# A fused two-layer transformer step: one attention key per query tile goes from TensorE to VectorE in layer 0's tiles 9 to 14

## What is computed

```python
scores = jnp.einsum('bqd,bkd->bqk', Qr, Kr) / jnp.sqrt(jnp.float32(d))
mask = jnp.tril(jnp.ones((T, T), dtype=bool), k=1)
scores = jnp.where(mask[None, :, :], scores, -jnp.inf)
attn = jax.nn.softmax(scores, axis=-1)
out = jnp.einsum('bqk,bkd->bqd', attn, V)
```

## Time and profile before

| | |
|---|---|
| median of 3 runs | 727.2 us (727.04 to 727.38) |
| profiled execution, its time | 725.66 us |
| its span in the trace | 723.9 us |
| PE busy | 640.5 us (88%) |
| PEld busy | 497.7 us (69%) |
| DVE busy | 473.1 us (65%) |
| ACT busy | 341.8 us (47%) |
| POOL busy | 225.4 us (31%) |
| granted TensorE clock, mean | 0.974 |

### The profile page before, as it was taken

One profiled execution on the slowest core, in us unless ns is written; L12 is line 12 of the kernel. 1 busy time (PEld: TensorE's weight loads), 2 busy tenths in 40 slices (PEclk: granted clock), 3 DMA queues, 4 the chain that ended last, 5 costly groups with the idle time before them and its releaser, 6 DMA issues.

```text
span 723.9 us, 10992 instructions
## 1 busy us (share of the span) xinstructions
PE 640.5 (88%) x3840; PEld 497.7 (69%) x3858; DVE 473.1 (65%) x1258; ACT 341.8 (47%) x705; POOL 225.4 (31%) x247
## 2 busy tenths in 40 slices
PE   5788899998878989988899998968889997899996
PEld 4356687877656778774668786846678885576774
DVE  5956499675767557726569776586744436766665
ACT  1133454565535464543445465443555552554553
POOL 3325545453544211004555445264410002000000
PEclk9979999999989999999999999998999999999999
DMA  8400000000000000000000000000000000001001
GB/s 261 117 1 1 1 2 1 1 2 0 1 1 1 0 1 1 1 1 1 1 0 2 0 1 1 1 1 1 1 1 1 2 2 0 1 15 30 15 24 34
DMA packets 12077, 9.64 MB, mean 13 GB/s; under 512 B 1708, under 2 KB 10744, under 8 KB 12024
## 3 DMA queue, kind: packets, MB, share of 16 engines
q1 hardware_dynamic: 12024, 8.94, 4.2%
HBM read 6.84 MB, written 2.10 MB: 12 GB/s over the span
## 4 chain that ended last, share of the span: by engine, by line
PE 65%; DVE 16%; ACT 8%; POOL 7%; issue 4%; DMA 1%; SPq 0%; POOLq 0%; ACTq 0%; DVEq 0%
PE ps L787 14%; PE ps L657 12%; PE ps L765 8%; PE ps L936 4%; PE ps L938 4%; PE ps L937 4%; PE ps L616 4%; PE ps L810 2%; PE ps L675 2%; PE ps L811 2%; PE ps L826 2%; ACT xn L1053 2%; DVE xn L1339 1%; PE ps L838 1%; DVE xn L1258 1%
## 5 line engine op out<-in xcount | busy, mean ns | idle before, releaser
L1113 ACT ACTIVATE probsT<-ps 128x512 f32<-128x512 f32 (+3 forms) x160 | 85.3, 533 | 172.1 <-PE ps L765 172.1
L787 PE MATMUL ps<-v_sb,probsT 128*128 128x129 f32 (+1 forms) x1148 | 157.1, 280 | 3.7 <-ACT probsT L1115 3.7
L787 PEld LDWEIGHTS ps<-v_sb,probsT 128*128 128x128 f32 (+1 forms) x1148 | 141.5, 191 | 10.7 <-ACT probsT L1115 5.6
L1376 DVE TENSOR_REDUCE row_max<-ps 128x1 f32<-128x512 f32 (+2 forms) x144 | 88.2, 620 | 61.3 <-PE ps L657 26.3
L765 PE MATMUL ps<-ident,probs 128*128 128x128 f32 (+1 forms) x574 | 92.6, 278 | 14.6 <-ACT hT L1043 7.8
L1087 ACT ACTIVATE probs<-ps,neg_max 128x512 f32<-128x512 f32 (+7 forms) x158 | 92.7, 617 | 15.8 <-DVE neg_max L1383 12.0
L765 PEld LDWEIGHTS ps<-ident,probs 128*128 128x128 f32 (+1 forms) x574 | 65.4, 139 | 45.6 <-issue 41.8
L515 POOL TENSOR_TENSOR hq<-ha,hp 128x352 f32<-128x352 f32 x32 | 29.9, 933 | 128.7 <-DVE hp L1419 128.7
L657 PE MATMUL ps<-k_high,q_high 128*128 128x512 f32 (+4 forms) x110 | 44.9, 408 | 2.3 <-ACT probs L1087 2.2
L1188 ACT ACTIVATE probs<-ps 128x512 f32<-128x512 f32 x40 | 24.0, 599 | 44.8 <-PE ps L938 44.8
L1391 DVE RECIPROCAL rsum<-ps 128x1 f32<-128x1 f32 x64 | 10.5, 165 | 50.3 <-PE ps L787 50.1
(11 more groups left out here) (243 smaller groups left out, 1376.7 us busy)
## 6 DMA issues: line engine op xcount, KB each, us to landing
out<-x_sb SPq DMA_DIRECT2D x8, 256.0 KB, 2.3
x_sb<-in_L_attn_x SPq DMA_DIRECT2D x2, 512.0 KB, 5.5
hT_all<-in_L_wmod SPq DMA_DIRECT2D x2, 384.0 KB
rope_cos<-table_cos SPq DMA_DIRECT2D x1, 768.0 KB, 6.8
rope_sin<-table_sin SPq DMA_DIRECT2D x1, 768.0 KB, 8.3
rope_cos<-table_cos SPq DMA_DIRECT2D x1, 256.0 KB, 3.6
rope_sin<-table_sin SPq DMA_DIRECT2D x1, 256.0 KB, 4.9
moe_raw<-in_L_ffn_expert_gate_w SPq DMA_DIRECT2D x1, 256.0 KB, 3.9
```

Source lines behind the costliest of these rows:

```text
L787: mm = pe.matmul(bank(OUT_AT, 0, V_W), probsT[0:size, n % 4, k * P:(k + 1) * P], v_sb[0:size, j, :], start=(c == 0 and k == 0), stop=(c == ...
L1113: ins = act.activation(probsT[:, n % 4, 0:full], bank(TURN, 0, full), ACT.Copy)
L1376: ins = dve.tensor_reduce(dst, ps[:, start:start + width], AX.X, ALU.max, negate=single)
```

## The change

For layer 0's tiles 9 to 14 (`edge_by_vector`; slots 9 to 14 of both batches, 12 in all) the key beyond the diagonal is no longer a tile of its own.

- Scores: where the last chunk is shorter than a bank (tiles 9, 10, 12, 13, 14) its three products and its mask product are two columns wider, and the four products of two columns go. Tile 11's last chunk fills its bank, so its four extra products stay.
- Turn and values: the transpose of one column, ScalarE's copy of one partition and the two products over one row go. Tile 11 has three chunks instead of four.
- finish(s) gets one VectorE instruction before the reciprocal: on partitions 96 to 127, value row times probability added to the accumulator in PSUM (129 columns), linked by a semaphore, and a wait for `v_edge_loaded`.
- The value rows lie on partition 127 of `v_edge`, a view of `moe_raw`, which GpSimd zeroes (128 x 1032 fp32) behind `first_rsqrt(2)`. SyncE moves them by four DMAs of one partition (2 KB), two for each batch, each behind a wait for the values and for the DMA before it.
- ScalarE waits for these DMAs before it puts layer 1's values over layer 0's (line 1011).
- SyncE's six loads of the experts' weights now stand behind these DMAs and behind layer 0's last tile of batch 1.

```diff
+EDGE_FROM = 9
+def edge_by_vector(layer, i):
+    return layer == 0 and EDGE_FROM <= i < TILES - 1
 def turn_chunks(layer, i):
     tiles = [(j, P) for j in range(i + 1)]
-    if layer == 0 and i < TILES - 1:
+    if layer == 0 and i < EDGE_FROM:
         tiles.append((i + 1, 1))
...
+            sp.wait_ge(edge_zeroed, 1)
+            for b in range(BATCH):
+                for g in range(EDGE_TILE // GROUP, GROUPS):
+                    sp.wait_ge(v_ready, b * 2 * GROUPS + g + 1)
+                    if b and g == EDGE_TILE // GROUP:
+                        sp.wait_ge(x_attn, (b - 1) * SLOTS + TILES)
+                    done = b * (GROUPS - EDGE_TILE // GROUP) + g - EDGE_TILE // GROUP
+                    if done:
+                        sp.wait_ge(v_edge_loaded, 16 * done)
+                    tiles = slice(g * GROUP - EDGE_TILE, (g + 1) * GROUP - EDGE_TILE)
+                    sp.dma_start(v_edge[P - 1:P, tiles, :], v_sb[0:1, g * GROUP:(g + 1) * GROUP, :]).then_inc(v_edge_loaded, 16)
+            EDGES = BATCH * (GROUPS - EDGE_TILE // GROUP)
+            sp.wait_ge(v_edge_loaded, 16 * EDGES)
+            sp.wait_ge(x_attn, (BATCH - 1) * SLOTS + TILES)
...
             first_rsqrt(2)
+            pool.memset(v_edge[:], 0.0).then_inc(edge_zeroed, 1)
...
-                mm = products(slice(start, start + full), not last)
+                beyond = 2 if width > full else 0
+                within = beyond if full < BANK and edge_by_vector(layer, i) else 0
+                mm = products(slice(start, start + full + within), not last)
                 if last:
-                    mm = pe.matmul(ps[:, start + full - P:start + full], ident_b[:],
-                                   (mask0, mask1)[layer][:, 0:P], start=False, stop=True)
-                    if width > full:
+                    mm = pe.matmul(ps[:, start + full - P:start + full + within], ident_b[:],
+                                   (mask0, mask1)[layer][:, 0:P + within], start=False, stop=True)
+                    if beyond > within:
...
+                if n % (2 * GROUPS) >= GROUPS:
+                    act.wait_ge(v_edge_loaded, 16 * (GROUPS - EDGE_TILE // GROUP) * (n // (2 * GROUPS) + 1))
                 act.wait_ge(v_proj_ready, n + 1)
...
                     acc = bank(OUT_AT, 0, V_W)
+                    if edge_by_vector(layer, i):
+                        per_batch = GROUPS - EDGE_TILE // GROUP
+                        dve.wait_ge(v_edge_loaded, 16 * (b * per_batch + (i + 1) // GROUP - EDGE_TILE // GROUP + 1))
+                        edge = acc[EDGE, :]
+                        link(dve.scalar_tensor_tensor(out=edge, in0=v_edge[EDGE, i + 1 - EDGE_TILE, :],
+                                                      scalar=probs[EDGE, s % 2, (i + 1) * P:(i + 1) * P + 1],
+                                                      in1=edge, op0=ALU.mult, op1=ALU.add))
                     link(dve.reciprocal(rsum[:, s % 2:s % 2 + 1], acc[:, P:V_W]))
```

More of the change, by code:

```diff
@@ L180, in build @@
         moe_raw = sb("moe_raw", [P, 3 * UNITS, P])
+        EDGE_TILE = EDGE_FROM // GROUP * GROUP
+        EDGE = slice(P - 32, P)
+        v_edge = moe_raw[:].rearrange("p n d -> p (n d)")[:, 0:(TILES - EDGE_TILE) * V_W].rearrange(
+            "p (t n) -> p t n", n=V_W)
         wv_s = sb("wv_s", [P, BATCH, P])
@@ L301, in build @@
         fp4_w_loaded = sem("fp4_w_loaded")
+        edge_zeroed = sem("edge_zeroed")
+        v_edge_loaded = sem("v_edge_loaded")
         moe_w_loaded = sem("moe_w_loaded")
@@ L659, in products @@
                     return mm
-                mm = products(slice(start, start + full), not last)
+                beyond = 2 if width > full else 0
+                within = beyond if full < BANK and edge_by_vector(layer, i) else 0
+                mm = products(slice(start, start + full + within), not last)
                 if last:
-                    mm = pe.matmul(ps[:, start + full - P:start + full], ident_b[:],
-                                   (mask0, mask1)[layer][:, 0:P], start=False, stop=True)
-                    if width > full:
-                        beyond = slice(start + full, start + full + 2)
-                        products(beyond, False)
-                        mm = pe.matmul(ps[:, beyond], ident_b[:], mask0[:, P:P + 2], start=False, stop=True)
+                    mm = pe.matmul(ps[:, start + full - P:start + full + within], ident_b[:],
+                                   (mask0, mask1)[layer][:, 0:P + within], start=False, stop=True)
+                    if beyond > within:
+                        alone = slice(start + full, start + full + 2)
+                        products(alone, False)
+                        mm = pe.matmul(ps[:, alone], ident_b[:], mask0[:, P:P + 2], start=False, stop=True)
                 mm.then_inc(scores_ready, 1)
```

## The result

| | before | after |
|---|---|---|
| median | 727.3 us (4 runs, 727.0 to 728.5) | 715.4 us (4 runs, 714.3 to 718.3) |
| profiled execution, its time | 725.66 us | 714.27 us |
| its span | 723.9 us | 712.4 us |
| mean granted TensorE clock in it | 0.974 | 0.978 |

The ratio of the times is 0.985 (95% interval 0.9825 to 0.9873): 11.9 us less, where 6.7 were forecast. In short: the work that the change takes off the path came out at 7.6 us, near the forecast 6.7; the rest, some 4 us, lies where TensorE spent less time at its lower clock, for which the forecast had allowed 1.7.

What follows compares the result with a forecast made beforehand. PE bounds the kernel (65% of what ended last), filling nearly all of slots 10, 11, 13 and 14. Two batches of 3.69 less, 0.65 more for the setup: 6.7 less, 727.2 to 720.5 us; range 718.2 to 723.6.

Steps and rivals of the forecast that it cites:

- Prices on PE: Work removed from PE: two-column score products 0.38 us, one-column turn 0.11, pair of one-row value products 0.51.
- The rival of cheap one-row products: Value products: one-row pair worth only its issue, 0.22 us instead of 0.51; 722.8 us in all, chance 0.12.
- Slots 8 and 9: No gain: VectorE still starts behind GpSimd's L507, so PE waits for xq at 118.06 whatever it saves.
- Slot 12: Gain of 0.42 us a batch; its value products hidden under normalise_2, VectorE's added instruction covered by up to 0.84.
- Slot 14: Net gain of 0.50 us a batch: 0.72 on PE less 0.22 because VectorE starts q_low late.
- The added instruction: VectorE in each finish: 0.35 us, bounds 0.28 and 0.69, plus 0.05 for link and wait.
- The memset: Setup: GpSimd's memset, about 0.88 us, blocks VectorE's L1295; 0.65 more taken, bounds 0 and 0.65.
- Moved loads, row DMAs: SyncE's moved expert loads cost zero; row DMAs come five slots early, so waits for them cost zero.
- The clock: Rival in layer 1's short slots: one TensorE clock fall more or fewer, 1.7 us, 719 to 722; chance 0.12.
- The rival on the slower side: Longer PE waits in slots 10 and 12 to 14 cost the clock: 6.8 to 13.6 us, up to 734.1; chance 0.06.

Runs made afterwards that it cites:

- e3: Changed kernel with the score products of before back in all tiles, so the values part alone; median 720.8 us, ratio 0.9905.
- e2: Kernel before with the score part alone (wider last chunks), value row still through TensorE; median 723.3 us, ratio 0.9956.
- e8: Changed kernel without VectorE's added instruction, the waits kept and the value row left out of the result; a single run, 713.9 us.
- e1: Changed kernel run again with no edit; median 714.7 us, ratio 0.9855.
- e7: Changed kernel with the memset moved ahead of first_rsqrt(1), where VectorE is idle; median 714.8 us, ratio 0.986.
- e12: Changed kernel with one setup instruction issued twice, to shift everything behind it by 1.36 us; median 716.9 us, ratio 0.9865.
- e6: Changed kernel with filling products in TensorE's idle times to hold the clock; median 711.6 us, ratio 0.980.
- e10: Changed kernel with clock-holding filling products, eight more ahead of slot 10, and the memset moved early; median 711.0 us, ratio 0.978.
- e11: Kernel before with one setup instruction issued twice, to shift everything behind it by 1.36 us; median 727.9 us, ratio 1.0007.
- e4: Kernel before with only the memset and SyncE's moved loads added; median 727.15 us, ratio 1.0001.
- e5: Kernel before with filling products in TensorE's idle times to hold the clock; median 717.95 us, ratio 0.990.

## Why the prediction was wrong, point by point

- **Prices on PE: right, a little low.** The end of slot 11 fell from 2.87 to 1.76, forecast 1.82. Slots 10, 11 and 13 came out at -0.81, -1.08, -0.98 for -0.72, -1.05, -1.00. Slots 10 and 14 each gave 0.08 to 0.09 more: fourteen products and the seam take 1.48 (124.80 to 126.28), 0.106 a step where I used 0.112. The rival of cheap one-row products (0.29 less gain in each of four slots) is refuted by e3's slot steps.
- **Slots 8 and 9: mis-sized, 0 instead of 0.25.** I asked only whether VectorE's conversion (line 1417 before, 1458 after) would get in before GpSimd, and it did not: 1.29 again. I overlooked what stands ahead of it. GpSimd's L507 took 1.52 because, it seems, the VectorE instruction ahead (L1414, from 106.58) ran beside its first part. After, VectorE is some 0.25 earlier against GpSimd, and the same GpSimd instruction takes 1.27. First DVE of before, then DVE and POOL of after, slot 8:

```profile
106.58 0.52 DVE L1414 SCALAR_TENSOR_TENSOR ha<-silu_g,qh 128x352 f32<-128x352 f32 x1
```

```profile
105.42 0.53 DVE L1455 SCALAR_TENSOR_TENSOR ha<-silu_g,qh 128x352 f32<-128x352 f32 x1
...
105.80 1.27 POOL L537 TENSOR_TENSOR xn<-xn,mod_row_now 128x512 f32<-128x512 f32 x1 [1.76 <-ACT xn L1087]
...
105.98 1.29 DVE L1458 TENSOR_SCALAR hp<-ha 128x352 int32<-128x352 int32 x1
```

  The 0.25 goes on through VectorE's wait and GpSimd's xq to PE. That L1414 is what lengthened it is argued from the overlap; e2 and e3 show that it comes with the scores part alone (1.27 in e2, 1.50 in e3). The wait ahead of slot 10 is 1.84 for a forecast 1.9.
- **Slot 12: mis-sized, -0.24 for -0.42.** I had called the added instruction covered there by up to 0.84. It was, but for the statistics' last step, which slipped behind the start of a GpSimd instruction and was held 0.33 longer; e8 gives 0.16 back. Also, the slots are not independent there, as the wait for ScalarE at slot 12's end takes back what slots 10 and 11 gave beyond the forecast: counted from slot 10, 2.19 were forecast up to there and 2.13 came.
- **Slot 14: mis-sized, -0.75 for -0.50.** q_low was to start 0.22 late. PE's wait grew by 0.11 (1.07 to 1.18) and 0.06 came back just ahead of it, so VectorE charged 0.05. The order of the queue was as described; the instructions ahead of q_low fitted better.

```profile
158.83 0.38 DVE L1429 SCALAR_TENSOR_TENSOR ps<-moe_raw,probs,ps 32x129 f32<-32x129 f32 x1
...
160.43 0.67 DVE L1410 TENSOR_REDUCE row_max<-ps 128x1 f32<-128x512 f32 x1
...
161.02 0.68 DVE L1507 SCALAR_TENSOR_TENSOR q_low<-ps,q_high 128x512 fp32r<-128x512 f32 x1
```

- **The added instruction: right.** 0.38 in all twelve places, for 0.35.
- **The memset: right in kind and size.** It took 0.96 for 0.88, and the tensor_scalar beside it 0.80 for a forecast 0.85, so it is no exception for writing only. That agrees with the rule of the Trainium skill ("SBUF — State Buffer", "Who interferes with whom"). The forecast's bound, 17.3 + 0.1 - 16.78, is 0.62 and not 0.65; 0.6 came.
- **Moved loads, row DMAs: right, nothing.** SyncE's longest wait on a row DMA was 1.1 us, and no other engine waited for one.
- **The clock: the step that failed.** The sum held no term for it, and the range allowed for one fall more or fewer, 1.7 us, in layer 1's slots. That was mis-sized. By the slots and the memset alone the time would have been 719.6, inside the range; the changed kernel came out another 3.1 us lower by the means of all runs and some 4 by the medians and by the two profiled executions. In those, the falls in the setup, at slot 18 and at the turn of the batches were moved, shorter or missing, worth about 4 us together, and in e1's those in the setup and at slots 18 and 25 of batch 1. Before's own 56 runs reach from a mean clock of 0.968 to 0.981, from 46 us at 1.2 GHz down to 27, so runs of one kernel already differ by more than one fall. Of the 5.1 us between forecast and median the slots are 0.8 (2 x 0.42).
- **The rival on the slower side: not borne out.** The wait ahead of slot 10 grew as it said, to 1.84, and yet none of the five profiles of the changed kernel and its variants without added filling products (the result's, e1, e7, e8, e12) has a fall in slots 9 to 14. With the clock held, e6 fell 1.7 us behind that wait, once, and not in batch 1. The falls in slot 13 (e6, e10) are no evidence for it, as e2 has them with the waits of before.
- **What stays open**: why the changed stream spends some 8 us less at 1.2 GHz on average. No experiment isolates a cause. e11 and e12 speak against its mere position in time, e4 against the setup part, and with the clock held the sign turns round (e5 13.3, e6 19.9). That the sign was to the good was luck as far as the forecast goes. e2 and e3 have about half of it each, within a spread that is as large.

## What to carry to other kernels

Take the falls of the granted clock into the forecast as a term with bounds of its own: list all of them in the profile of before, price each by what one costs where PE is late (here 1.3 to 1.65 us for 3.4 us), and let the range hold several coming and going, in stretches that the change does not touch too. Compare kernels by the fixed points of the bound engine, slot by slot: that gave the change's own worth to 0.1 us while the medians still moved by several. When an instruction is moved by a few tenths on VectorE, look for GpSimd instructions whose start it passes: each such passing changed a duration here by 0.25 to 0.6 us, in either direction.

## What the runs showed of the hardware that I had not expected

- A write-only GpSimd memset holds up a VectorE tensor_scalar for its whole length: 0.20 became 0.79 to 0.80 beside it, and 0.20 again with the memset elsewhere.
- Two instructions that both go on seem to slow one another (argued from the overlap alone): GpSimd's 128 x 512 product took 1.52 with VectorE's scalar_tensor_tensor beside its first 0.4 us and 1.27 where they overlapped by 0.15.
- One and the same kernel, e2, ran in 717.8 and in 727.9 us, with mean granted clocks of 0.981 and 0.965. A fill that held the clock in the kernel before (runs within 1.2 us) left the changed one, with less work and longer waits, a spread of 5.7.
